# A gated layer stack on one core: the dense mix spread over three engines, the single-head attention in plain fp32, and the routing of each expert layer's second half moved ahead of its loop

## What is computed

```
x += g * attention16heads(ln(x), ctx)      # run 0 of heads8, head width 8
x += g * experts_top2(ln(x))               # run 0 of experts: 8 experts, 2 per token, hidden 512
x += g * attention16heads(ln(x), ctx)      # heads64, head width 64
x += g * mix(ln(x))                        # mixed: all 8 experts, weights from a softmax cut at 0.1
x += g * attention1head(ln(x), ctx)        # head128
x += g * experts_top1(ln(x))               # run 1 of experts
x += g * attention16heads(ln(x), ctx)      # run 1 of heads8
x += g * ternary_mlp(ln(x))                # ternary
# mix: out = sum_e w[:, e] * (h @ W[e] + b[e]);  w = softmax(h @ gate_w + gate_b), below 0.1 dropped, renormalised
```

## Time and profile before

| | |
|---|---|
| median of 3 runs | 997.49 us (996.33 to 1000.16) |
| profiled execution | 996.21 us, its span 994.4 us |
| mean granted PE clock | 0.847 of full |
| busy share of the span | PE 77%, DVE 52%, ACT 38%, POOL 28% |

### The profile page before, as it was taken

How to read it: one execution, slowest core, us unless ns; L and a number is a source line. 1 busy time by engine, 2 the same in 40 slices (tenths; PEclk the granted TensorE clock), 3 DMA queues, 4 the chain that set the end, 5 groups by cost and what they waited for, 6 DMA issues and landing times.

```text
span 994.4 us, 18119 instructions
## 1 busy us (share of the span) xinstructions
PE 767.9 (77%) x6805; PEld 652.2 (66%) x6805; DVE 519.3 (52%) x1610; ACT 378.3 (38%) x886; POOL 278.8 (28%) x229
## 2 busy tenths in 40 slices
PE   4789872878959898989997556994486975988874
PEld 3567750777858787979786334774374964767764
DVE  5467461352234776666664878424242333778562
ACT  5455530333424654646461001210132554555450
POOL 4344316514332450212020000000305334344031
PEclk9999795798979999999998877555596986999996
DMA  7533625525733000000001000000432634321001
GB/s 182 131 89 104 195 74 172 136 73 162 208 102 102 19 23 1 2 1 2 1 1 64 0 1 0 1 1 28 147 97 85 181 105 118 104 64 34 1 12 32
DMA packets 60546, 70.95 MB, mean 71 GB/s; under 512 B 7036, under 2 KB 40717, under 8 KB 60461
## 3 DMA queue, kind: packets, MB, share of 16 engines
q1 hardware_dynamic: 57389, 63.48, 22.6%
q0 software_dynamic: 3072, 6.30, 2.1%
HBM read 48.86 MB, written 20.91 MB: 70 GB/s over the span
## 4 chain that ended last, share of the span: by engine, by line
PE 53%; DVE 19%; issue 8%; DMA 7%; ACT 6%; POOL 6%; SPq 0%; POOLq 0%; DVEq 0%; ACTq 0%
PE banks L1346 6%; PE banks L1362 5%; PE banks L1027 4%; PE banks L1438 4%; POOL xs L648 4%; DMA xs<-xn,slot 3%; PE banks L1028 3%; PE banks L1029 3%; DVE x L2221 3%; PE banks L1447 3%; PE banks L1069 3%; PE banks L1458 3%; PE banks L1155 3%; PE banks L1178 2%; PE banks L1167 2%
## 5 line engine op out<-in xcount | busy, mean ns | idle before, releaser
L898 ACT ACTIVATE hT<-banks,wup 128x128 f32<-128x128 f32 x304 | 85.6, 371 | 155.4 <-PE banks L1346 139.2
L1346 PE MATMUL banks<-xTs,wup 128*128 128x128 f32 x608 | 95.2, 309 | 21.2 <-issue 12.9
L1346 PEld LDWEIGHTS banks<-xTs,wup 128*128 128x128 f32 x608 | 88.1, 223 | 25.0 <-issue 24.9
L573 POOL TENSOR_TENSOR kbd<-k,const 96x1248 fp32r<-96x1248 f32 x32 | 72.3, 2266 | 70.4 <-PE banks L1155 68.2
L815 ACT ACTIVATE pT<-banks 77x512 f32<-77x512 f32 x128 | 69.0, 589 | 57.8 <-PE banks L1155 57.7
L1362 PE MATMUL banks<-wd,hT 128*128 x608 | 87.7, 292 | 3.8 <-ACT hT L898 3.8
L556 POOL TENSOR_TENSOR rstd<-vv,const 128x4 f32<-128x4 f32 x24 | 24.3, 1014 | 223.0 <-DVE vv L1662 223.0
L1362 PEld LDWEIGHTS banks<-wd,hT 128*128 128x128 f32 x608 | 81.1, 208 | 4.3 <-issue 4.2
L648 POOL DMA_INDIRECT xs<-xn,slot x48 | 46.5, 969 | 121.8 <-DVE slot L1960 89.8
L2072 DVE COPY ysb<-banks 128x128 f32<-128x128 f32 x76 | 22.0, 289 | 107.9 <-PE banks L1362 93.1
L611 POOL TENSOR_TENSOR sh<-sh,rd 128x616 f32<-128x616 f32 x32 | 38.9, 1216 | 129.4 <-DVE rd L1715 128.8
(11 more groups left out here) (323 smaller groups left out, 1787.3 us busy)
## 6 DMA issues: line engine op xcount, KB each, us to landing
wup<-in_up SPq DMA_DIRECT2D x76, 258.0 KB
q<-queries SPq DMA_DIRECT2D x24, 256.0 KB, 4.3
queries<-qc SPq DMA_DIRECT2D x8, 512.0 KB, 2.7
wd<-in_down SPq DMA_DIRECT2D x8, 512.0 KB, 5.1
ys<-ysb SPq DMA_DIRECT2D x16, 256.0 KB
k<-keys SPq DMA_DIRECT2D x24, 156.0 KB, 3.6
xs<-zt SPq DMA_DIRECT2D x2, 1472.0 KB, 11.5
keys<-kc SPq DMA_DIRECT2D x8, 312.0 KB, 3.4
```

The source lines that it names most:

```text
L573: pool.tensor_tensor(kbd[b % NB8][0:96, :, :, :].bitcast(F32R), kb, m, ALU.mult).then_inc(h8.kbd, 1)
L898: ins = act.activation(hT[T % 3][:, c, :], ps[:, T % 2, c * P:c * P + P], func, bias=wup[T % NW][:, HID + c:HID + c + 1])
L1346: ins = pe.matmul(ps[:, T % 2, c * P:c * P + P], w_[:, c * P:c * P + P], xTs[T % 3][:, :], start=True, stop=True)
```

## The change

It has five parts.

1. **Mix.** PE makes each unit by one plain fp32 matmul from an fp32 transposed x (`xT`, kept twice, even and odd groups), and the gate's scores too; no `xlo` is made. Of each batch's two units ACT multiplies the first quad of experts by its weights into `mtmp` (`products`), DVE does the second quad into x as before, and POOL adds the four products, the bias and x (`mixed_sum`). ACT scales the front's tokens. The gate of group 0 and the first two units are put inside the last group of heads64.
2. **head128.** `q2` and `k2` are plain fp32, the scores, transposed scores and query product one matmul each; k and v products stay split. On PE the next front stands ahead of the transposed scores, on DVE `outputs` comes one group later.
3. **Half 2 is routed in head128**: statistics, `norm8` and `turn` of half 2 in its last two steps, `logits` and `ranks` behind it.
4. **Halves 1 and 3 are routed ahead of the loops**; in the loop stay `weigh`, `bias8` and `combine`, the latter at tiles 10, 11 and 19, 20. In heads8 of run 0 the routing of half 0 begins at b = 8 and `slots(0)` stands at b = 16.
5. **Indirect DMAs.** Scatters of halves 0 and 2 are issued without a wait between them, with the next half's `token_roots` among them. Each scatter of half 1 or 3, and each gather of half 0 or 2, waits for one more finished tile of the running loop (`mo.ye`).

```diff
@@ spread and collect, POOL
-                if hh:
-                    token_roots(hh)
...
                 for k_ in range(chosen(hh)):
                     for t in range(HT):
-                        if t % 4 == 0 and k_ * HT + t:
-                            pool.wait_ge(mo.scat, moves(hh) + 16 * (k_ * HT + t))
+                        m = k_ * HT + t
+                        if hh % 2 == 0 and m == 4 * chosen(hh):
+                            token_roots(hh + 1)
+                        if hh == 0 and m == 12:
+                            length_roots(1)
+                        if hh % 2:
+                            pool.wait_ge(mo.ye, BASE[hh - 1] + 1 + m)
...
+                    if hh % 2 == 0:
+                        pool.wait_ge(mo.ye, BASE[hh + 1] + 1 + m)
@@ mixed, POOL
+            def mixed_sum(g):
+                m = mtmp[g % 2]
+                pool.wait_ge(mx.act, 4 * (g + 1))
+                pool.tensor_tensor(m[:, :, 0:2, :], m[:, :, 0:2, :], m[:, :, 2:4, :], ALU.add).then_inc(su.plink, 1)
...
+                pool.tensor_tensor(m[:, :, 0, :], m[:, :, 0, :], m[:, :, 1, :], ALU.add).then_inc(su.plink, 1)
...
+                pool.wait_ge(mx.xb, g + 1)
+                pool.tensor_tensor(m[:, :, 0, :], m[:, :, 0, :], m[:, :, 4, :], ALU.add).then_inc(su.plink, 1)
...
+                pool.wait_ge(mx.half, 4 * (g + 1))
+                xt = x[:, GB * g:GB * g + GB, :]
+                pool.tensor_tensor(xt, xt, m[:, :, 0, :], ALU.add).then_inc(mx.x, 1)
@@ mixed, ACT
+                for g in range(NG):
+                    n = g + 3 * NG + 1
+                    scaled(next_group(g), n)
+                    products(g, 0)
+                    act.wait_ge(mx.ct_mm, g + 1)
+                    copy(cT[:, 0, :], ps[0:GB * E, 6, 0:P]).then_inc(mx.ct, 1)
+                    products(g, 1)
+                    front(n)
+                    products(g, 2)
+                    act.wait_ge(mx.b_mm, g + 1)
+                    copy(mtmp[g % 2][:, :, 4, :], ps[:, 6, :].rearrange("p (t d) -> p t d", t=GB)).then_inc(mx.xb, 1)
+                    if g < NG - 1:
+                        gate_exp(g + 1)
+                    products(g, 3)
@@ mixed, DVE
+                for g in range(NG):
+                    n = g + 3 * NG + 2
+                    weighted(g, 0)
+                    front_a((g + 2) % NG, n)
+                    weighted(g, 2)
+                    if g < NG - 1:
+                        mixed_gate(g + 1)
+                        front_b((g + 2) % NG, n)
+                        mixed_weights(g + 1)
@@ head128, PE
-                        split3(ps[:, 0, :], tuple(w_[:, 0, :] for w_ in w2), xs).then_inc(h1.qmm, 1)
+                        pe.matmul(ps[:, 0, :], b_raw[:, 0:P], xT[g % 2], start=True, stop=True).then_inc(h1.qmm, 1)
...
+                        if g == NG:
+                            turn(2, 0)
+                            turn(2, 1)
...
+                logits(2)
+                ranks(2)
@@ experts, DVE, ahead of the loop
+                wait_done(dve, "h1" if run else "h8", 1)
+                stats8(hh + 1, 0)
+                stats8(hh + 1, 1)
+                variance8(hh + 1)
+                weigh(hh, gate)
                 bias8(hh, 0)
+                norm8(hh + 1, 0)
+                norm8(hh + 1, 1)
                 bias8(hh, 1)
+                for part in range(4):
+                    route(hh + 1, part)
+                slots(hh + 1)
@@ experts, DVE, loop of the second half
-                            if 6 <= i < 6 + 2 * chosen(hh):
-                                combine(hh - 1, (i - 6) // 2, i % 2)
+                            if i in (10, 11):
+                                combine(hh - 1, 0, i - 10)
+                            if run == 0 and i in (19, 20):
+                                combine(hh - 1, 1, i - 19)
```

More of the change, by code:

```diff
@@ L212, in build @@
         assert wregion[0] <= back_at
+        wregion = [top[0], wend]
+        mtmp = [place(f"mtmp{i}", [P, GB, 5, D], F32, wregion) for i in range(2)]
         wregion = [top[0], wend]
@@ L307, in build, with split_upto @@
         back_in = (mo.gat0, mo.gat1)
-        ON_ACT = (*range(0, NG), *range(6 * NG, 7 * NG + 1))
+        ON_ACT = (*range(0, NG), *range(3 * NG + 1, 4 * NG + 1), *range(6 * NG, 7 * NG + 1))
+        PLAIN = (*range(3 * NG, 5 * NG),)
+        xT = (xT_even[:, :], xT_odd[:, :])
+        def split_upto(n):
+            return sum(m not in DROPPED and m not in PLAIN for m in range(n + 1))
         def shifts(n):
@@ L694, in _ @@
             ins.then_inc(su.scratch, 1)
-            for g in range(0, NG):
-                rsqrt_front(g + 4 * NG + 1)
+            for g in range(NG):
+                rsqrt_front(g + 3 * NG + 2)
+                mixed_sum(g)
+            for g in range(0, NG - 1):
+                rsqrt_front(g + 4 * NG + 2)
+            token_roots(2)
             spread(2)
@@ L862, in heads8 @@
                         front(NG * phase + g + 2)
-                    if run == 0 and b == 14:
+                    if run == 0 and b in (11, 12):
+                        turned(0, b - 11)
+                    if run == 0 and b == 15:
                         tanh(0)
-            def first_norm(a_):
-                act.wait_ge(mo.nn, 1)
-                for t in range(GB * a_, GB * a_ + GB):
-                    ins = act.activation(xn8[0][:, t, :], x[:, t, :], ACT.Identity, bias=mb8[:, t:t + 1],
-                                         scale=rstd8[:, t:t + 1])
-                ins.then_inc(mo.xn, 1)
             def turned(hh, a_):
@@ L1242, in heads8 @@
                         gate_rows(0)
-                    if run == 0 and b == 11:
-                        turn(0, 1)
+                    if run == 0 and b in (11, 12):
+                        turn(0, b - 11)
+                    if run == 0 and b == 13:
+                        logits(0)
+                    if run == 0 and b == 15:
+                        ranks(0)
                     if run and b == 9:
@@ new lines, in mixed, with weighted @@
+            def mixed():
+                def weighted(g, t0):
+                    for e in range(4):
+                        for t in (t0, t0 + 1):
+                            if e == 0:
+                                dve.wait_ge(mx.o, 8 * g + 2 * t + 2)
+                            else:
+                                lk.wait(back=0 if e == 3 and t > t0 else 1)
+                            xt = x[:, g * GB + t, :]
+                            ins = dve.scalar_tensor_tensor(out=xt, in0=ps[:, (8 * g + 2 * t + 1) % 6, e * P:e * P + P],
+                                                           scalar=cw8[:, GB * (g % 2) + t, 4 + e:5 + e], in1=xt,
+                                                           op0=ALU.mult, op1=ALU.add)
+                            if e < 3:
+                                lk.mark(ins)
+                            else:
+                                ins.then_inc(mx.half, 1)
+                wait_done(dve, "h64", 1)
+                front_b(1, 3 * NG + 1)
+                dve.wait_ge(mx.c, 1)
+                for g in range(NG):
+                    n = g + 3 * NG + 2
[6 more added lines that the diff above has]
+                        mixed_weights(g + 1)
+                        dve.wait_ge(mx.c, g + 2)
```

435 lines of the change are left out of this document (194 added, 241 removed).

## The result

The changed kernel takes 914.19 us (median of 4 runs, 913.09 to 921.48) against 996.91 before: ratio 0.9181, 95% interval 0.9129 to 0.9233. That is inside the predicted range of 860 to 925 and 27 us above the forecast of 887. The profiled execution has a span of 911.3 us, 83.1 less than before; the forecast was 110.4 less.

A forecast was written before the change was run, and what follows sets the result against it. The prediction took the loops to be held by DVE's list, not PE, and the mix by DVE alone; its terms summed to −110.4 us, a span of 884.0, forecast 887 us relative to the median, range 860 to 925.

The forecast's parts named there:

- What bounds the loops: Expert loops: held by DVE's list, not PE; at 1.90 us a tile loop 0 falls 44 us to 96.
- rival 2: Loops become bound by something not PE, weights or DVE's copies, at 2.4 us a tile: 925 us; chance 0.12.
- The start: Start of loop 0: +12.5 us, first scatter some 10 us later, first tile 36 us after it; bounds +8 and +16.
- The indirect DMAs one by one: Scatters and gathers tied to single tiles: 0 us, since spread under 10 to 20 tiles of PE work.
- heads64: heads64 stage: +3 us, of it +2.4 waits at its start, +0.6 score calls for the mix; bounds 0 and +5.
- The mix: Mix: −30.6 us, four groups of 12 us plus a 2.5 us tail, 50.5 against 81.1; bounds 42 and 60.
- Rival 1: Half clock through head128, port conflicts in the mix: 15 us a group (+12), head128 57 us (+9), 908 us; chance 0.20.
- head128: head128 stage: −15 us to 48, between 57 at half clock and 41 at full clock; bounds 40 and 57.
- the stage behind it: From head128's end to loop 1's first tile: −5 us, 33.5 against 38.6; bounds 29 and 37.
- Loop 1: Second expert loop, 30 tiles at 1.90 us: −32.3 us, 67.5 against 99.8; bounds 63 and 75.
- The hold by POOL's work: Mix: POOL's SBUF sums can hold small DVE instructions; 1 us allowed within 12 a group, about 15 if full.
- rival 4: Slower than before: weight stream with indirect DMAs sets the tile; loses from 3.65 us a tile, 1,005 at 3.75; chance 0.02.

The follow-up runs named there:

- late_split: The changed kernel with POOL's three splittings of heads64's weights moved from behind half 0's scatters to behind half 1's: 904.71 us, ratio 0.9036.
- units_home: The changed kernel with the mix's first two units back at the mix's start, not between heads64's last two batches: 919.12 us, ratio 0.9193.
- weights_first: The changed kernel with DVE making the next group's gate and weights before adding the current group's second half: 905.85 us, ratio 0.903.
- five: Changed kernel with late_split, early_zero, weights_first, and POOL's mix sums held until the next group's weights, the last group's until DVE scaled the next front: 886.01 us, ratio 0.891.
- old_gathers: The changed kernel with first halves' gathers issued and added as before the change, all routing still ahead of the loops: 931.62 us, ratio 0.9343.
- early_zero: The changed kernel with POOL's zeroing of k moved ahead of the root of heads64's first front: 912.6 us, ratio 0.9121.

## Why the prediction was right, and where it fell short

The time is inside the range, and most signs that the prediction named were there: the first tile at 186.5 us (183 to 190), tiles in steps of 1.90, both loops near the forecast. Two were not: the first tile came 40.4 us after the first scatter (33 to 38), and a group of the mix took 17.6 us, where the prediction had called itself wrong from 14 on.

- **What bounds the loops** was right: with routing and waiting additions out of DVE's list, tiles run at 1.90 us. Loop 0 took 97.4 us from its first tile to its last product (186.5 to 283.9); the term said 96, and the DMA share was 0.59, where rival 2 had reckoned with 0.72. What it lacked is most of the 7.9 us behind it, for which the forecast had 2.4 (its waits at the start of heads64).
- **The start** (+12.5, measured +12.1) was right by luck: two errors cancelled. The first scatter came 5 us later instead of 10, and the routing of half 1 took 40.4 us instead of 36. The term priced DVE's choice by undisturbed rows although POOL's splitting stood beside it in the order; without it, it takes 31.6 (late_split).
- **The indirect DMAs one by one** were priced at 0. They are worth 3 to 5 us each (gathers 5.1, scatters 4.6 against the changed kernel) in loop 0, and 2.8 in loop 1 (gathers). Together with the place of the additions, the gathers' part is 15.5 of loop 0's 35.2. The forecast of the loop was near the truth because 1.90 a tile silently assumed this.
- **heads64** (+0.6 for the scores) is mis-sized: +8.0 in the profiled execution, +4 to +6 in the variants. The two units that the change puts there, 3.7 us at low clock, are part of the change and were not in the term; whether they are what is missing, units_home does not show.
- **The mix** (−30.6, measured −18.8) is the step that failed most, "12 a group". Busy times were nearly right (in a group of 17.6 us PE 11.7 at a clock of 0.79, and 10.0 at the full clock in weights_first; DVE 11.3 with 3.0 of holds in it; ACT 7.4, POOL 7.1), but I closed the group by a guess for hand-overs and did not walk its chain: last addition, gate, exponent, weights, next units, all on DVE behind `weighted(g, 2)`, and in it POOL's sums. Rival 1 had the hold (3 us a group; measured 2.33 + 1.12 less 0.4, 3.0) but set it on top of 12, so even its 15 was short.
- **head128** (−15, 48 us) and the stage behind it (−5) were right: 48.8 us, and −6.2. Its clock was 0.79, between the two levels as taken, but the reason I gave, that denser work in the mix keeps it up, is contradicted: weights_first and five, with a group of the mix or all of it at 1.00, have 0.68 and 0.67 behind it, head128 and routing together, where the change has 0.76. And 48.8 was partly luck: units_home and old_gathers, with the same code for head128, took 62.5 and 59.4 us up to the first scatter of half 2, where the change took 57.7.
- **Loop 1** (−32.3, measured −27.3) is mis-sized by 5: of 73.5 us, 70.9 go up to the last product (the term said 67.5 in all) and 2.6 are a wait for the front. No run shows which part of the term was short.
- **The hold by POOL's work** was weighed, with the earlier trace rows, for the mix alone. The same two rows, asked of every POOL instruction that the change sets beside new DVE work, would have given the splitting (8.8) too. The zeroing (3.7) does not follow from them: the DVE instruction that it held has one tile in, and only early_zero shows that case.
- **A slip in rival 4**: outside the loops the terms add up to 34.1 us saved, not "about 37", so the loss begins at 3.6 us a tile and 3.75 a tile gives some 1,008. The forecast does not rest on it.

In all, five, which removes most of the holds and mends the order, is at 886.01 us, where the prediction had put the change itself (887). That agreement is mostly luck, since its terms do not agree: against the forecast for each stage it is 10.0 us early at the first tile and 9.3 below in the mix, and above it by 3.4 in loop 0, 5.3 in heads64, 7.7 from head128 to the first scatter of half 2, and 4.2 in loop 1.

## What to carry to other kernels

When a change moves work on one engine, look at what stands at that time on the other engines. Here POOL's sums and splittings made DVE instructions of 0.2 us last 0.9 to 2.3 us, and the zeroing made four scalings of 1.1 us last 4.8. Such passes did no harm beside DVE's copies out of PSUM. For a loop over groups, walk the chain that closes one group into the next, in the order of each engine's list; the largest busy time told 10.5 us where the chain took 17.6. Beside this stream of weights the indirect DMAs cost less one by one than in fours (3 to 5 us less in a loop of 105), although no engine is busier for it.

## What was not expected of the hardware

- A zeroing on POOL (4.25 us) held a DVE `tensor_scalar` from SBUF to SBUF, four of them 4.84 us where 1.12 is usual, but not four `scalar_tensor_tensor` with two SBUF inputs, 1.13 us in its midst.
- A faster mix was followed by a slower clock: head128 with routing took 57.7 us at 0.76 behind the mix of 63.0, and 60.5 and 63.8 us at 0.68 and 0.67 behind mixes of 47.8 and 41.9 (in the second, 1.7 us of it is idle time of PE). In units_home it took 62.5 at 0.69 behind a mix of 64.4, and in old_gathers 59.4 at 0.72 behind 61.9, so the length of the mix is not the cause. What decides it is open.
